# Softmax weights times values in a decoder block: the exponentials as the stationary operand, the division on token partitions

## The reference

```python
q = x_q @ W_q.T + b_q
k = x_kv @ W_k.T + b_k
v = x_kv @ W_v.T + b_v
qh, kh, vh = (_split_heads(q), _split_heads(k), _split_heads(v))
scores = jnp.einsum('bhqd,bhkd->bhqk', qh, kh) * scale
attn = jax.nn.softmax(scores, axis=-1)
ctx = jnp.einsum('bhqk,bhkd->bhqd', attn, vh)
ctx = ctx.transpose(0, 2, 1, 3).reshape(x_q.shape[0], x_q.shape[1], D)
return ctx @ W_out.T + b_out
```

## Time and profile before

| | |
|---|---|
| median of 3 runs | 719.36 us (718.80 to 720.44) |
| the profiled execution | 719.91 us, span 718.1 us |
| mean granted TensorE clock | 0.989 |
| busy: TensorE (matmuls) / weight loads | 673.4 us (94%) / 494.7 us (69%) |
| busy: VectorE / ScalarE / GpSimd | 631.8 us (88%) / 372.8 us (52%) / 353.1 us (49%) |

### The profile page before, as it was taken

One profiled execution on the slowest core, in us unless ns is written; L12 is line 12 of the kernel. 1 busy time (PEld: TensorE's weight loads), 2 busy tenths in 40 slices (PEclk: granted clock), 3 DMA queues, 4 the chain that ended last, 5 costly groups with the idle time before them and its releaser, 6 DMA issues. The chain is left out here.

```text
span 718.1 us, 12542 instructions
## 1 busy us (share of the span) xinstructions
PE 673.4 (94%) x4396; PEld 494.7 (69%) x4412; DVE 631.8 (88%) x1257; ACT 372.8 (52%) x720; POOL 353.1 (49%) x491
## 2 busy tenths in 40 slices
PE   9889999999989998899979899899999999999995
PEld 3478765887747886468866686567777876666663
DVE  4998787999989999989999788558999997999997
ACT  3732157021264502464112723679767776988885
POOL 0633424646045761258431561580692223788785
PEclk9999999999999999999989999999999999999999
DMA  8630045321331536143382077810000000000012
GB/s 308 180 60 1 0 118 112 74 50 28 61 58 31 131 109 71 23 78 79 113 113 64 1 194 136 298 56 2 2 2 2 2 2 1 1 31 31 31 60 89
DMA packets 35112, 50.31 MB, mean 70 GB/s; under 512 B 4744, under 2 KB 29192, under 8 KB 34794
## 3 DMA queue, kind: packets, MB, share of 16 engines
q0 software_dynamic: 7680, 16.77, 14.9%
q1 hardware_dynamic: 26506, 31.95, 13.4%
q10 hardware_dynamic: 864, 0.79, 0.4%
HBM read 29.59 MB, written 7.34 MB: 51 GB/s over the span
## 5 line engine op out<-in xcount | busy, mean ns | idle before, releaser
L705 ACT ACTIVATE yb<-banks 128x256 f32<-128x256 f32 x64 | 24.2, 386 | 156.9 <-PE banks L427 110.5
L450 PE MATMUL banks<-xt_in,w_in 128*128 128x512 f32 x192 | 87.8, 611 | 0.2
L418 PE MATMUL banks<-inv_m,spec_y 128*128 128x256 f32 x384 | 86.8, 383 | 0.0
L375 PE MATMUL banks<-z_cplx,fwd_m 128*128 128x256 f32 x240 | 72.3, 383 | 9.7 <-DVE prod L1078 5.4
L418 PEld LDWEIGHTS banks<-inv_m,spec_y 128*128 128x128 f32 x384 | 74.2, 193 | 10.3
L376 PE MATMUL banks<-z_cplx,fwd_m 128*128 128x256 f32 x240 | 71.4, 379 | 0.0
L450 PEld LDWEIGHTS banks<-xt_in,w_in 128*128 128x128 f32 x192 | 36.7, 194 | 42.8 <-issue 39.5
L375 PEld LDWEIGHTS banks<-z_cplx,fwd_m 128*128 128x128 f32 x240 | 44.8, 190 | 18.9 <-issue 8.4
L376 PEld LDWEIGHTS banks<-z_cplx,fwd_m 128*128 128x128 f32 x240 | 45.7, 191 | 6.1
L2016 DVE TENSOR_REDUCE peak<-ps_score 128x16 f32<-128x1024 f32 x32 | 38.2, 1194 | 8.2 <-PE ps_score L1501 8.2
L1742 ACT ACTIVATE silu<-ps_score,gate_back 128x1024 f32<-128x1024 f32 x32 | 35.6, 1113 | 18.7 <-issue 17.6
(11 more groups left out here) (292 smaller groups left out, 1725.0 us busy)
## 6 DMA issues: line engine op xcount, KB each, us to landing
x_tok<-in_x SPq DMA_DIRECT2D x8, 512.0 KB, 4.4
x_tok<-in_b_out POOLq DMA_DIRECT2D x8, 512.0 KB, 13.3
v_t<-left POOLq DMA_DIRECT2D x8, 511.5 KB, 4.6
x_t<-left POOLq DMA_DIRECT2D x8, 511.5 KB, 5.3
xt_in<-in_x_t SPq DMA_DIRECT2D x3, 1024.0 KB, 5.9
x_scratch<-x_tok SPq DMA_DIRECT2D x6, 512.0 KB, 4.1
x<-x_scratch SPq DMA_DIRECT2D x6, 512.0 KB, 9.3
out<-x SPq DMA_DIRECT2D x6, 512.0 KB, 2.9
```

The costliest lines, as they stand in the source:

```text
L375: mm(o, fwd_m[:, at + 2 * half + odd, :], zz[:, 0, :], start=True, stop=False)
L418: last = mm(bank[:, odd * 2 * P:(odd + 1) * 2 * P], spec_y[:, j + odd, part * D + h * P:part * D + (h + 1) * P], inv_m[:, o:o + 2 * P], st ...
L450: last = mm(proj_pair(b, t)[:, c * 512:(c + 1) * 512], w_in[:, k, TILES[t] * P:(TILES[t] + 1) * P], xt_in[:, k, c * 512:(c + 1) * 512], st ...
```

## The change

The work behind `turn_prob` goes tile by tile and with the operands exchanged. `values(j)` has a 128x128 block of `prob_t` stationary (two heads' exponentials, context tokens on partitions, tokens as columns) and the values of the two heads moving, 32 columns and two columns of ones (`v_pairs` has 34 columns a pair now; two memsets write the ones). The result, token partitions, is 8 x 34 columns of a PSUM bank: the contexts and, in the two last columns, the sums of the exponentials. `divide(j)` on VectorE takes the reciprocals of the 16 sums and multiplies 256 columns with them into `c_n`. `turn_context(j)` turns it, two transposes; ScalarE copies 256 columns to `c_t` (`evac_context`); `project(j)` and `add_residual(j)` are as before, for one tile. `sums`, `spread_inverses`, `invert`, `evac_inverses` and `normalize` go, with the constants `key_head` and `spread` and their two loads. Two PSUM banks take turns, and `prob_t` has four buffers of one tile instead of two of a pair.

The peaks of `x2` in the loop are taken once for four tiles (`x_peaks`), from tile 15 on. Queues: TensorE has `scores(j+1)`, `turn_context(j-4)`, `turn_prob(j)`, `values(j-3)`, `project(j-4)`; VectorE `shift(j)`, `divide(j-4)`, `add_residual(j-5)`; ScalarE the exponentials, `evac_context(j-4)`, `evac_prob(j)`, `square(j-6)`.

```diff
-            def sums(i):
-            def spread_inverses(i):
...
-            def values(i):
-                if i:
-                    pe.wait_ge(added, i)
+            def values(j):
+                pe.wait_ge(pt_evac, j + 1)
+                if j < 2:
+                    pe.wait_ge(q_evac, DT * (CHUNKS - Q_EARLY) - 1 + j)
                 else:
-                    pe.wait_ge(q_evac, DT * (CHUNKS - Q_EARLY))
-                b = 2 * i * P // L
+                    pe.wait_ge(added, j - 1)
+                b = j * P // L
                 for t in range(DT):
                     for r in range(STRIPS):
-                        last = mm(ps_ctx[r * STRIP:(r + 1) * STRIP, t * 2 * P:(t + 1) * 2 * P],
-                                  v_pairs[:, b, t * STRIPS + r, :], prob_t[:, i % 2, r * DT + t, :], start=True, stop=True)
+                        p = t * STRIPS + r
+                        last = mm(ctx_bank(j)[:, p * PAIR:(p + 1) * PAIR], prob_t[:, j % T_BUFS, r * DT + t, :],
+                                  v_pairs[:, b, p, :], start=True, stop=True)
                 last.then_inc(pv_mm, 1)
...
+            def turn_context(j):
+                pe.wait_ge(c_divided, j + 1)
+                for t in range(DT):
+                    last = transpose(ctx_bank(j)[:, t * P:(t + 1) * P], c_n[:, j % 2, t * P:(t + 1) * P], ident[:])
+                last.then_inc(c_turned, 1)
+
+            def project(j):
+                pe.wait_ge(ct_ready, j + 1)
+                for t in range(DT):
+                    last = mm(ctx_bank(j)[:, D:2 * D], c_t[:, j % 2, t * P:(t + 1) * P], wo[:, t, :],
+                              start=(t == 0), stop=(t == DT - 1))
                 last.then_inc(wo_mm, 1)
...
+                if j >= 4:
+                    turn_context(j - 4)
                 turn_prob(j)
...
+                if j >= 3:
+                    values(j - 3)
+                if j >= 4:
+                    project(j - 4)
+            pe.wait_ge(ident_ready, 1)
+            pe.wait_ge(pt_evac, TILES_ALL)
+            turn_input(0)
+            turn_context(LAST - 3)
             pe.wait_ge(shifted, TILES_ALL)
             pe.wait_ge(w_seq, 9)
             inner(0, ps_gate, w_gate, silu_done, gate_mm)
+            values(LAST - 2)
+            project(LAST - 3)
             inner(0, ps_up, w_up, h_ready, up_mm)
             turn_input(1)
-            project(HALVES - 2)
-            spread_inverses(HALVES - 1)
...
+            def evac_context(j):
+                act.wait_ge(c_turned, j + 1)
+                if j >= 2:
+                    act.wait_ge(wo_mm, j - 1)
+                fn(c_t[:, j % 2, :], ctx_bank(j)[:, 0:D], ACT.Copy).then_inc(ct_ready, 1)
...
+            dve.wait_ge(v_zero, 1)
+            for r in range(2):
+                nc.vector.memset(v_pairs[r * NCTX:(r + 1) * NCTX, :, :, 2 * DH + r:2 * DH + r + 1], 1.0).then_inc(v_ready, 1)
...
+            def divide(j):
+                dve.wait_ge(pv_mm, j + 1)
+                contexts = ctx_bank(j)[:, 0:PAIRS * PAIR].rearrange("p (a n) -> p a n", n=PAIR)
+                inverse = inv_sum[:, j % 2, :].rearrange("p (a r) -> p a r", r=2)
+                recip(inverse, contexts[:, :, 2 * DH:]).then_inc(inverted, 1)
+                dve.wait_ge(inverted, j + 1)
+                if j >= 2:
+                    dve.wait_ge(c_turned, j - 1)
+                tt(c_n[:, j % 2, :].rearrange("p (a r n) -> p a r n", r=2, n=DH),
+                   contexts[:, :, 0:2 * DH].rearrange("p a (r n) -> p a r n", r=2),
+                   inverse.unsqueeze(3).broadcast_to([P, PAIRS, 2, DH]), ALU.mult).then_inc(c_divided, 1)
...
+                if j >= 4:
+                    divide(j - 4)
+                if j >= 5:
+                    add_residual(j - 5)
...
-                    if k == CH - 1:
-                        x_scales(c)
...
+                if c in range(X_EARLY) and k == 0:
+                    x_peaks(c)
+                    x_scales(c)
...
+            add_residual(LAST - 4)
+            divide(LAST - 3)
+            divide(LAST - 2)
             dve.wait_ge(w_seq, 9)
             for s in range(LAST):
                 hidden(s)
...
+                if s in (1, 2):
+                    divide(LAST - 2 + s)
+                if s < 4:
+                    add_residual(LAST - 3 + s)
```

More of the change, by code:

```diff
@@ L113, in shape_constants @@
     pair_mask = np.repeat((row // DH % 2)[:, None] == np.arange(2), NCTX, axis=1)
[L114 to L119, removed]
     out = {
         "c_fwd": fwd.reshape(P, -1), "c_inv": inv, "c_pe": pe_t, "c_negt": neg_t,
-        "c_ident": np.eye(P), "c_pairmask": pair_mask, "c_keyhead": key_head.reshape(P, -1),
-        "c_spread": spread.reshape(P, -1),
+        "c_ident": np.eye(P), "c_pairmask": pair_mask,
     }
@@ L1280, in attention_operands @@
     pair_mask = small[:, o:o + 2 * NCTX].rearrange("p (h n) -> p h n", n=NCTX)
[L1281 to L1286, removed]
+    assert o + 2 * NCTX <= DT * 3 * D
+    return w, ctx_t, ctx_2, pair_mask, bo, bv, bk
 def query_weights(left):
@@ L1652, in _ @@
                 if s == 0:
-                    values(HALVES - 1)
+                    values(LAST - 1)
+                    project(LAST - 2)
                 if s == 1:
-                    project(HALVES - 1)
+                    turn_context(LAST - 1)
+                    values(LAST)
+                    project(LAST - 1)
+                if s == 2:
+                    turn_context(LAST)
                 if s - 3 in tiles:
                     if s == 3:
-                        pe.wait_ge(added, HALVES)
+                        pe.wait_ge(added, TILES_ALL)
                     down(s - 3)
@@ L1709, in evac_prob, with square @@
                 act.wait_ge(pt_mm, j + 1)
[L1710 to L1712 removed]
+                if j >= T_BUFS:
+                    act.wait_ge(pv_mm, j - T_BUFS + 1)
+                fn(prob_t[:, j % T_BUFS], ps_pt[:].rearrange("p (h n) -> p h n", n=P),
                    ACT.Copy).then_inc(pt_evac, 1)
[L1715 to L1729, removed]
+            def evac_context(j):
[3 more added lines that the diff above has]
+                fn(c_t[:, j % 2, :], ctx_bank(j)[:, 0:D], ACT.Copy).then_inc(ct_ready, 1)
+            def square(j):
+                act.wait_ge(added, j + 1)
+                c, k = j // CH, j % CH
+                act.wait_ge(squared, j) if j else act.wait_ge(l_squared, 2 * CH)
+                if c >= 2:
+                    act.wait_ge(floored, c - 1)
+                fn(spread_sq[:], x2[:, j, :], ACT.Square, scale=-float(D), bias=row_sum[:, c % 2, k:k + 1],
+                   accum_out=row_var[:, c % 2, k:k + 1]).then_inc(squared, 1)
             def evac_input(i):
@@ L1779, in _ @@
                     evac_q(Q_EARLY + 2)
[L1780 to L1783, removed]
+                if j >= 6:
+                    square(j - 6)
             evac_input(0)
+            evac_context(LAST - 3)
             fn(table_of[:, 1:2], bk[:, 0:1], ACT.Silu)
@@ L2036, in add_residual @@
-            def add_residual(i):
-                dve.wait_ge(wo_mm, i + 1)
-                dve.wait_ge(biased, 2 * i // CH + 1)
-                for k in range(2):
-                    j = 2 * i + k
-                    c, m = j // CH, j % CH
-                    if c >= 2 and k == 0:
-                        dve.wait_ge(squared, CH * (c - 2) + m + 2)
-                        dve.wait_ge(centred, c - 1)
-                    last = stt(x2[:, j, :], ps_ctx[:, k * D:(k + 1) * D], 1.0, x2[:, j, :], ALU.mult, ALU.add,
-                               accum_out=row_sum[:, c % 2, m:m + 1])
-                last.then_inc(added, 1)
+            def divide(j):
[9 more added lines that the diff above has]
+                   inverse.unsqueeze(3).broadcast_to([P, PAIRS, 2, DH]), ALU.mult).then_inc(c_divided, 1)
@@ new lines, in add_residual, with x_peaks @@
+            def add_residual(j):
+                dve.wait_ge(wo_mm, j + 1)
+                c, k = j // CH, j % CH
+                dve.wait_ge(biased, c + 1)
+                if c >= 2:
+                    dve.wait_ge(squared, CH * (c - 2) + k + 1)
+                    dve.wait_ge(centred, c - 1)
+                stt(x2[:, j, :], ctx_bank(j)[:, D:2 * D], 1.0, x2[:, j, :], ALU.mult, ALU.add,
+                    accum_out=row_sum[:, c % 2, k:k + 1]).then_inc(added, 1)
+            def x_peaks(c):
+                dve.wait_ge(x2_ready, c + 1)
+                of = slice(c * CH, (c + 1) * CH)
+                reduce(x_peak[:, of], x2[:, of, :], AX_X, ALU.max, apply_absolute_value=True).then_inc(x_peaked, CH)
```

106 lines of the change are left out of this document (30 added, 76 removed).

## The result

The changed kernel takes 737.41 us in the median of 4 runs (736.51 to 739.85) beside 719.17 us for the kernel before on the same chip: a ratio of 1.0256, 95% interval 1.0228 to 1.0283, 18.2 us more. Its profiled execution has a span of 735.7 us, 17.6 more than before.

The account below looks back on a forecast made before the run. TensorE's time per tile was taken as the bound, VectorE close behind. Loop +14.3 us (+15.3, start -1.0) and tail +4.5 made +18.8 on a median of 719.36: 738.5 us said, 730 to 750 for 8 in 10.

Parts of the forecast that it names:

- The bound: Attention stage: TensorE's time per tile decides, 4.0 us a tile before; VectorE is the second limit, close behind.
- Values, 16 x 0.111 = 1.78 us: Values on TensorE, per tile: 16 loads of 128 f32 columns, each priced with its move at 0.111 us.
- The choice among 0.032, 0.111 and 0.14: Price in us of a load with its move in the values: sums' 32-column pace, full load, or load and move in turn.
- Contexts 0.26, turning 1.02, projection 0.87: TensorE, us per tile: two transposes of the contexts, turning the exponentials, and the projection, unchanged per tile.
- the rival by which the turning's 0.13 us would be won (735 us): Turning in the loop: part of its 1.02 us is a wait that slack engines remove, -3.6 us; 10%.
- Loop +15.3: Turning of tile 3 to that of tile 31: 127.9 us against 112.6, at 4.59 us a tile.
- Start -1.0: Ahead of tile 3's turning: the sums of pair 0 go, 1.0 us less.
- Tail +4.5: Behind the last turning: first hidden product 3.1 us later, fifth 4.5 later, with nothing to win it back.
- The new waits: TensorE's waits for the division and ScalarE's copy cost nothing; rival that they bite: 0.3 us a tile, +8, 747 us, 10%.
- Loads hidden, 713.6 us: Rival: values' loads run side by side at 0.032 us, TensorE needs 3.3 us a tile, VectorE decides; 5%.
- The clock: Rival: TensorE's clock falls to 1.2 GHz in the loop, about 865 us; 2%, as the new loop has no idle time.

Follow-up runs that it names:

- e1: Changed kernel with each product of the values moving up to three pairs, 102 columns instead of 34, the excess overwritten by the next: 737.14 us.
- e2: Changed kernel with moving operands of the values as wide as possible, 34 columns for the first pair up to 272 for the eighth: 756.2 us (one run).
- e4: Changed kernel in f32 with each block of exponentials loaded as four blocks of 32 columns into the four column groups: 712.77 us, ratio to before 0.9905.
- e6: Changed kernel with the turned exponentials and the values (`prob_t`, `v_pairs`) in bf16, the rest f32: 710.72 us, ratio 0.9874.
- e3: Changed kernel with every product of the values issued twice, so twice the loads and moves: 823.72 us (one run).
- e5: Changed kernel with every product of the values issued twice and moves of 102 columns in place of 34: 795.35 us (one run).
- e9: Changed kernel with the peaks of x2 taken one tile at a time from tile 12 on, in place of five grouped ones: 738.86 us, ratio 1.0278.

## Why the prediction was right

I had said 738.5 us, in 730 to 750; 737.4 came. Point by point:

- *The bound.* TensorE before and after, as the chains show.
- *Values, 16 x 0.111 = 1.78 us.* 1.71, one load in 0.107. The choice among 0.032, 0.111 and 0.14 was the step on which all hung; the earlier trace rows decided it, and e1, e2, e4 and e6 show that it was the load.
- *Contexts 0.26, turning 1.02, projection 0.87.* 0.37, 0.87 and 0.94. The first two trade places: the group that follows the scores pays about 0.15 us more (the two transposes take 0.37 us there and 0.22 behind other products in the tail), and that is now the contexts'. So the rival by which the turning's 0.13 us would be won (735 us) didn't come. The sum was 4.59 and is 4.55.
- *Loop +15.3.* +14.1 by the timeline from turning to turning. 28 tiles at 4.55 instead of 4.59 are 1.1 of the difference. Three more errors offset each other: the last tile has no scores of a next one ahead of its turning, which the sum left in (it takes 3.83 us, -0.7); the weight-sum product adds 0.1 and not 0.3; and tile 16 is 0.6 us late, the first tile 0.2 longer than said.
- *Start -1.0.* Only -0.2. This term was wrong: the sums of pair 0 stood in TensorE's queue where it waits anyway. In the changed kernel's chain ScalarE's last query copy and the exponentials come last there, and TensorE waits for them:

```profile
479.09 1.08 PE L1503 MATMUL ps_pt<-ident,prob 128*128 128x128 f32 x8 [0.73 <-ACT prob L1690]
```

- *Tail +4.5.* +4.53, +3.16 of it ahead of the first hidden product (+3.1 said), with the idle 1.04 us for the division (1.1 said) and nothing won back behind it. Here too a part is luck: the wait for the residual of tile 28 is 0.41 us and not 0.8, and 0.48 us of waiting for ScalarE's copy of the input, which no term had, stand ahead of it. In the whole sum errors of -1.2 in the loop and +0.8 at the start nearly cancel, so the time came closer than its terms.
- *The new waits.* None of them holds the loop; the first turning of contexts waits 0.2 us for its division, the others in the loop not at all. The one tile that is late, tile 16 with 5.18 us, has another cause, told at the end.
- *Loads hidden, 713.6 us.* Not so in the changed kernel. e4 makes the loads overlap and takes 712.8, e6 makes them cheap and takes 710.7. That e4 comes so near the rival's time is partly luck: its loop is 7.0 us shorter than before where 4.8 was said, its start 0.2 where 1.0 was, and its tail is 0.9 longer where none was.
- *The clock.* It held. That I gave 2% because the loop isn't idle was argued from too little: e3 shows it falling in a loop that never idles. The reading of the earlier trace rows was wrong as well, for the clock of the kernel before also fell where TensorE had not been idle almost half the time (0.83, busy 8.35 of 10 us):

```profile
300.00:310.00 10.00, 8.35 (x27) 4.67 (x28) 7.59 (x10) 5.23 (x8) 4.77 (x5) 0.83 0.55 105
```

## What to carry to other kernels

Before making the larger operand stationary, count weight loads, not only columns moved: an f32 product has two, each of 128 columns costs 0.107 us, and with 34 or 102 moving columns that is all the product costs. Column groups (e4) or bf16 (e6) take that price away, and only then does the work saved on other engines count. Before an edit is credited with work taken off a queue, look whether the queue waits at that place anyway.

## What was unexpected

A TensorE that is not idle can be granted half its clock for stretches: 0.76 is the mean of a 40 us window of e3, against 1.00 with the same loads and moves of 102 columns in e5 (one execution each).

A VectorE instruction of 4 columns that usually takes 0.17 us took 0.83 in the changed kernel, and it was the stall at tile 16. VectorE's and GpSimd's timelines:

```profile
533.92 0.83 DVE L2046 TENSOR_SCALAR x_unit<-x_peak 128x4 f32<-128x4 f32 x1
```

```profile
532.82 1.91 POOL L1865 TENSOR_SCALAR w_raw<-w_raw 128x2048 f32<-128x2048 f32 x1
```

It ended at 534.75, GpSimd's at 534.73. In e9 it took 1.64 us and ended at 535.80, with GpSimd's at 535.78; in the kernel before it took 0.41 and ended at 527.28, GpSimd's at 527.25. Its 0.66 us too many are the 0.63 that tile 16 is late; behind the later groups of peaks of the loop it takes 0.17 and the tiles 4.55. The maxima and subtractions around it, and the reciprocal of the same 4 columns (0.18 us), ran beside GpSimd undisturbed. That it waits for GpSimd is read from these three ends; no run took GpSimd's instruction away. The Trainium skill has a row on this (GPSIMD Engine Reference, section "1. Specifications": GpSimd's SBUF interfaces are shared with VectorE, and instructions in a 2-port mode or with two SBUF inputs contend), and the three ends agree with a shared interface; this instruction has one input, and no run here shows its mode.
